# Masking the second score pass of a fused attention tower on GpSimd instead of TensorE

## The reference, cut to what matters

```
# token layer, 4 times (band: a query sees keys within W = 64 positions)
scores = where(allowed, q.k / sqrt(16), -1e9);  probs = softmax(scores);  a = probs @ v
h = layer_norm(h + a @ Wo + bo);  h = layer_norm(h + gelu(h @ W1 + b1) @ W2 + b2)
# causal attention on layer_norm(h): q and k rotated, then
att = where(key <= query, q.k / 4, -inf);  y = softmax(att) @ v;  h = h + y @ W_proj + b_proj
# experts: top-k by gate score, silu(x Wg) * (x Wu) @ Wd, scattered and added; plus the shared branch
```

## Time and profile before

| what | value |
|---|---|
| median of three runs | 7495.74 us (7485.59 to 7497.77) |
| profiled execution, its own time | 7492.35 us |
| span of its trace | 7490.6 us, mean granted TensorE clock 0.967 |
| PE busy | 6488.7 us, 87% of the span |
| DVE busy | 4520.8 us, 60% |
| ACT busy | 2636.2 us, 35% |
| POOL busy | 1088.9 us, 15% |
| DMA | 25 GB/s over the span |

### The profile page before, as it was taken

One profiled execution on the slowest core, in us unless ns is written; L12 is line 12 of the kernel. 1 busy time (PEld: TensorE's weight loads), 2 busy tenths in 40 slices (PEclk: granted clock), 3 DMA queues, 4 the chain that ended last, 5 costly groups with the idle time before them and its releaser, 6 DMA issues. The chain is left out here.

```text
span 7490.6 us, 145369 instructions
## 1 busy us (share of the span) xinstructions
PE 6488.7 (87%) x54482; PEld 4986.5 (67%) x54482; DVE 4520.8 (60%) x11626; ACT 2636.2 (35%) x4677; POOL 1088.9 (15%) x1089
## 2 busy tenths in 40 slices
PE   1999999999999999999999999978888886279999
PEld 1777777777777777777777777756666664256766
DVE  6666666666666666666666666656666665732222
ACT  0444444444444444444444444433333332001111
POOL 4000000000000000000000000011111110133333
PEclk9999999999999999999999999989999998589999
DMA  5000000100000100000000000000000000023332
GB/s 99 15 14 14 14 14 14 29 14 14 14 14 14 29 14 14 14 14 14 19 25 14 14 14 14 14 28 17 17 16 18 16 17 17 0 61 84 69 83 52
DMA packets 195770, 185.94 MB, mean 25 GB/s; under 512 B 44402, under 2 KB 181268, under 8 KB 195668
## 3 DMA queue, kind: packets, MB, share of 16 engines
q1 hardware_dynamic: 168020, 147.84, 6.6%
q0 software_dynamic: 27648, 36.72, 3.1%
HBM read 124.23 MB, written 60.26 MB: 25 GB/s over the span
## 5 line engine op out<-in xcount | busy, mean ns | idle before, releaser
L684 ACT ACTIVATE pT<-bank 128x384 f32<-128x384 f32 x1920 | 857.9, 489 | 1184.0 <-PE bank L509 1184.0
L861 DVE TENSOR_REDUCE mx<-bank 128x2 f32<-128x384 f32 x1548 | 813.1, 554 | 497.5 <-PE bank L483 497.5
L481 PE MATMUL bank<-maskb,eyeb 128*128 128x384 bf16 x1932 | 641.9, 332 | 197.0 <-DVE mx L861 67.7
L578 PE MATMUL bank<-hT,w 96*128 96x256 f32 x3072 | 770.9, 387 | 43.5 <-ACT hT L704 43.5
L507 PE MATMUL bank<-maskb,eyeb 128*128 128x384 bf16 x1920 | 634.9, 331 | 54.6 <-ACT pT L684 49.2
L483 PE MATMUL bank<-kT,qT 128*128 128x192 bf16 (+2 forms) x3864 | 638.5, 247 | 0.0
L509 PE MATMUL bank<-qT,kT 128*128 128x192 bf16 (+2 forms) x3840 | 629.3, 246 | 0.0
L578 PEld LDWEIGHTS bank<-hT,w 96*128 96x128 f32 x3072 | 542.6, 190 | 125.4 <-ACT hT L704 72.6
L468 PE MATMUL bank<-eyeb,stack 128*128 128x128 bf16 x7728 | 541.1, 227 | 70.3 <-DVE stack L847 70.3
L468 PEld LDWEIGHTS bank<-eyeb,stack 128*128 128x128 bf16 x7728 | 489.6, 102 | 104.1 <-DVE stack L847 80.7
L590 PE MATMUL bank<-w,pT 128*128 128x192 f32 x3072 | 533.5, 330 | 0.0
(11 more groups left out here) (203 smaller groups left out, 11160.0 us busy)
## 6 DMA issues: line engine op xcount, KB each, us to landing
hcur<-hbuf SPq DMA_DIRECT2D x165, 192.0 KB, 2.4
hbuf<-hout SPq DMA_DIRECT2D x128, 192.0 KB, 2.0
amb<-am_d SPq DMA_DIRECT2D x131, 128.0 KB, 2.9
exp_wg<-in_ewg SPq DMA_DIRECT2D x16, 768.0 KB
exp_wu<-in_ewu SPq DMA_DIRECT2D x16, 768.0 KB
exp_wd<-in_ewd SPq DMA_DIRECT2D x16, 576.0 KB
xs<-xr SPq DMA_DIRECT2D x32, 272.0 KB, 2.2
hbuf<-emb_z SPq DMA_DIRECT2D x17, 384.0 KB
```

Of the source, the lines that this page charges most:

```text
L481: nc.tensor.matmul(dst[:, 0:SCOLS], eyeb[:], maskb[:, masks, :], start=True, stop=False)
L578: last = nc.tensor.matmul(bank[s][f // 2][:, (f % 2) * S:(f % 2 + 1) * S], w1[:, c, f * P:(f + 1) * P], hT[s][:, c, :], start=(c == 0), st ...
L684: ph.inc(nc.scalar.activation(pT[s][:, h % NPT, :], bank[s][h % 2][:, 0:SCOLS], ACT.Exp, scale=SCALE), "p", s)
L861: last = nc.vector.tensor_reduce(mx[s][:, :, h], src[:, 0:SCOLS].rearrange("p (t k) -> p t k", t=T), AX, ALU.max)
```

## The change

The mask matmul of the second pass goes, in both kinds of layer, so the two score matmuls open and close their own accumulation. The exponential is then also taken of scores that are masked, relative to a maximum over the unmasked ones. On POOL a new function `pool_keep` zeroes the masked entries of `pT` in place, for four heads at a time, with `affine_select`, an instruction that compares an affine expression of partition and column with zero and keeps the entry or writes 0.0. For a band group these are four instructions (64, 128, 128 and 64 columns, times four heads); for a causal group two (128 columns, times four heads). Three groups stand between POOL's front part (L1045) and its rstd (L1050). A new key "kept" counts groups, and `pe_products` waits for it in place of "p". In the order of PE the products are set later: group 0 after head 8, group 1 after head 11, group 2 between fill 1 and fill 2, and the output transposes between fill 3 and fill 4. The number of slots of `pT` (8), the banks, the first score pass and its mask matmuls stay.

```
-            nc.tensor.matmul(dst[:, 0:SCOLS], eyeb[:], maskb[:, masks + 1, :], start=True, stop=False)
             for t, (c0, f0, w) in enumerate(kcols):
                 last = nc.tensor.matmul(dst[:, c0:c0 + w], kT[s][:, h, t * P:(t + 1) * P],
-                                        qT[s][:, h, f0:f0 + w], start=False, stop=(t == T - 1))
+                                        qT[s][:, h, f0:f0 + w], start=True, stop=True)
...
-            ph.wait(pe, "p", s, K.it, 4 * g + 4)
+            ph.wait(pe, "kept", s, K.it, g + 1)
...
-                if K and h >= 3 + LAG and (h - 3 - LAG) % 4 == 0:
-                    pe_products(ph, pe, K, (h - 3 - LAG) // 4, kcols)
+                if K and h in (8, 12):
+                    pe_products(ph, pe, K, h // 4 - 2, kcols)
             for f in range(6):
                 if K and f == 2:
+                    pe_products(ph, pe, K, 2, kcols)
+                if K and f == 4:
                     pe_output(ph, pe, K)
...
+        def pool_keep(ph, pool, K, g, causal):
+            s = K.s
+            ph.wait_apart(pool, "p", s, K.it, 4 * g + 4, half_ok, 1)
+            pool.wait_ge(half_ok, 1)
+            p = pT[s][:, (4 * g) % NPT:(4 * g) % NPT + 4, :]
+            def keep(x, n, w, key, base):
+                return nc.gpsimd.affine_select(x, x, [[0, n], [-key, w]], ALU.is_ge, 0.0, base=base, channel_multiplier=key)
+            if causal:
+                keep(p[:, :, 0:P], 4, P, -1, 0)
+                last = keep(p[:, :, 2 * P:3 * P], 4, P, -1, 0)
+            else:
+                keep(p[:, :, 0:W], 4, W, -1, W)
+                keep(p[:, :, W:3 * W], 4, P, 1, 0)
+                keep(p[:, :, 3 * W:5 * W], 4, P, -1, 0)
+                last = keep(p[:, :, 5 * W:6 * W], 4, W, 1, 0)
+            ph.inc(last, "kept", s)
...
             if K:
+                for g in range(3):
+                    pool_keep(ph, pool, K, g, causal)
                 s = K.s
                 ph.wait(pool, "var1", s, K.it)
```

More of the change, by code:

```diff
@@ L414, in tower @@
             h_in=16, hT_ps=1, hT=1, qk_ps=2, v_ps=1, qk=2, v=1, stk=1, fill=6, ev_v=3, ev_s=3,
-            sc1=NH, mx=NH, m=1, mT_ps=3, mT=3, sc2=NH, p=NH, pv=NH, ot=1, otT_ps=2, att=1,
+            sc1=NH, mx=NH, m=1, mT_ps=3, mT=3, sc2=NH, p=NH, kept=3, pv=NH, ot=1, otT_ps=2, att=1,
             aT_ps=1, aT=1, wo_ps=1, var1=1, rstd1=1, h1=1, h1T_ps=1, h1T=1)
@@ L497, in pe_maxima, with pe_scores2 @@
                 ph.inc(last, "mT_ps", s)
-        def pe_scores2(ph, pe, K, h, masks, kcols):
+        def pe_scores2(ph, pe, K, h, kcols):
             s = K.s
@@ L633, in tensor_half @@
                 if K and h < NH:
-                    pe_scores2(ph, pe, K, h, masks, kcols)
+                    pe_scores2(ph, pe, K, h, kcols)
                 if F and h == plan.input:
```

## The result

The changed kernel takes 8074.48 us, median of four runs (8065.84 to 8083.34), against 7493.85 us before; the ratio is 1.0776, 95% interval 1.0758 to 1.0795. The forecast was 8095 us. Its profiled span is 8064.1 us, 573.5 us more than before.

What follows compares the result with a forecast made beforehand. PE, busy 87% of the span, was taken as the bound, with DVE's stack chain nearly tied. 2.3 + 1.4 + 0.6 us a token half gave 550 us, the causal layer 48: 8095 us, range 7600 to 8650.

Steps and rivals of the forecast that it cites:

- The floor: Token half with masks that cost nothing: first score at t = 17.27 against 17.48, a gain of 0.2 us, not 2.0.
- K: Time of POOL's four selects for one band group (1536 elements a partition): 2.8 us, range 1.6 to 4.0.
- The chain by t: Token half: group 0 kept at 7.7, group 2 starts at 13.4, first score 6.35 us later at 19.75, 2.3 us late.
- Contention: Token half: POOL's keeps and DVE operations with two SBUF inputs hold each other up, 1.4 us, bounds 0 and 2.7.
- Clock: Token half: PE's granted clock falls after standing ahead of groups 0 and 2, costing 0.6 us, from 0 up to 2.3.
- Sum of the token layers: 2.3 + 1.4 + 0.6 = 4.3 us a token half, x 128 = 550 us slower.
- The causal layer: Group 0 starts at 10.1, group 2 at about 15.4; fills already late, so 1.5 us a half (0.5 to 3), 48 us.

Runs made afterwards that it cites:

- no_keep: The changed kernel without its affine selects, products waiting for the exponentials, late order kept; 7521.08 us, ratio 1.0043 to the kernel before.
- keeps_first: The changed kernel with the three keeps ahead of the front's residual on POOL; 8180.01 us, ratio 1.0971 to the kernel before.
- keeps_aside: The changed kernel with the selects working on a separate tile that no product waits for; 8176.54 us, ratio 1.0915 to the kernel before.
- pow_wait: The changed kernel with each group's selects replaced by tiny POOL powers, PE still waiting for them; 8010.94 us, ratio 1.0694 to the kernel before.
- quarter_keeps: The changed kernel with each select on one head of its four, same instructions and waits; 7532.01 us, ratio 1.0101 to the kernel before.
- warm_first: The changed kernel with 8 idle matmuls ahead of PE's wait for group 0; 8137.01 us, ratio 1.0854 to the kernel before.
- two_heads: The kernel before, early order, with only heads 0 and 1's second-pass masks moved to one early POOL keep; 7432.88 us, ratio 0.9920 to before.

## Why the prediction was right, and where it wasn't

**The floor** (a gain of 0.2 us a token half at best): right, and along the forecast's own path. `no_keep` shows 0.01 for the half; its fill 0 starts at t = 9.84 (9.85 forecast), product group 2 at 10.84 (10.92) and the first score at 17.15 (17.27).

**K.** Forecast 2.8 us a band group, without contention. Measured 2.43 for the third group of the half shown and 2.93 for the first two (5.85 / 2), but both lie beside DVE's work; a group that DVE nearly leaves alone takes 2.18 us (`keeps_first`, group 0). Single selects with nothing of DVE beside them take about 0.23 us for 64 elements, 0.29 for 128, 0.41 for 256 and 0.63 for 512: 0.9 ns an element and a fixed 0.18 us. So the fixed 0.2 us read off the adds was right and the 1.3 ns an element was too much. That the whole came near the contended group is luck, for the forecast then added contention on top. (The Trainium skill's "roughly line-rate" for one input, "GPSIMD Engine Reference", section 4.1, gave 2.1 us; the undisturbed group agrees to 4%.)

**The chain by t.** Group 0 forecast for 7.8, measured 7.97; group 2 forecast for 13.4 plus a contention of 1.4, measured 14.02; from there to the first score 6.35 forecast, 6.31 measured. That path, read off rows 4 and 5 gap by gap, was the most exact part of the sum, at full clock; in the other kind of half it takes 6.82 us.

**Contention.** The mechanism is shown by `keeps_aside` and `pow_wait`; the bookkeeping wasn't right. I let only DVE operations with two SBUF inputs stand against POOL, but the casts (741 against 561 ns) and above all the small bf16 copies (413 against 253) stretch as well: of 1.8 us that the stack chain grew in the half shown, 0.64 are those of the six copies (1.74 us in its timeline against 1.10). And I added it to POOL's chain alone. It is on both: by the undisturbed 2.18 us a group, POOL's three groups grew by 1.7 us in the half shown (5.85 + 2.43 against 6.54), and DVE's chain by 1.8. In the other kind of half DVE's chain is the one that PE meets, which the forecast has no path for. Because the two chains end so close together, one sum for either came out about right, and that is luck too. (The Trainium skill, "SBUF — State Buffer", section "SBUF: two separate sides", counts VectorE instructions in a 2-port mode among those that contend with GpSimd, and says that whoever comes second blocks for the whole instruction. The records agree: the copies of `keeps_aside` that begin under a select end 0.11 to 0.12 us after it. In the change 413 ns is a mean of copies that met one, up to 709 ns, and of others that fell into POOL's pause; the median is 254.)

**Clock.** 0.6 us forecast. Up to the first score the half shown lost 2.85 us and the other kind 3.76. Behind fill 0 the clock takes 1.3 us of the latter and nothing that can be read of the former, 0.65 on average. The stretch at 0.50 ahead of fill 0 is not in that, so the whole is somewhat more. The mean half lost 3.68; what is missing from 3.3, the mean of the two, lies mostly behind the first score and isn't explained.

**Sum of the token layers.** 4.3 forecast, 3.68 measured: 550 against 471 us.

**The causal layer is the step that failed.** I took 1.5 us a half, with bounds of 0.5 and 3; it is 3.27. The first score comes at t = 23.33 against 20.05. The timeline in the changed kernel (t = 0 at 5703.06) answers to the earlier trace rows:

```profile
5711.17 4.07 POOL L1042 TENSOR_SCALAR_AFFINE_SELECT pT<-pT 128x512 f32<-128x512 f32 x4
...
5713.18 1.51 PE L526 MATMUL bank<-pT,vaug 128*32 128x256 f32 x16 [3.22 <-POOL pT L1042]
...
5716.63 1.97 DVE L846 COPY stack<-stack 128x384 bf16<-128x384 bf16 x6
...
5718.79 1.89 PE L468 MATMUL bank<-eyeb,stack 128*128 128x128 bf16 x16 [1.14 <-DVE stack L848]
...
5720.60 1.51 PE L526 MATMUL bank<-pT,vaug 128*32 128x256 f32 x16
```

Group 0 comes at t = 10.1, as forecast. But I reasoned that the fills are late anyway and would swallow the rest. The stack chain, which makes them late, is itself held up by the selects: fill 0 starts at t = 15.73 in place of 13.79. And product group 2, which used to run ahead of PE's wait for that chain, now stands behind it and behind fills 0 and 1, at half clock: from 5720.60 to the next fill at 5722.05 it is 1.4 us of path where it was free. 1.9 + 1.4 = 3.3. But that the second term is the step's is an account of this one half. `quarter_keeps` has the same order, and its causal half corrects it:

```profile
5714.96 1.07 PE L468 MATMUL bank<-eyeb,stack 128*128 128x128 bf16 x16 [0.35 <-DVE stack L848]
...
5715.95 0.86 PE L526 MATMUL bank<-pT,vaug 128*32 128x256 f32 x16
```

Fill 0 starts at t = 13.78, where it did before, PE has not stood long ahead of it, and the granted clock is at 1.00 all through the fills. The moved step is 0.8 us of path (5715.95 to 5716.74), and still the first score starts at t = 19.91, 0.14 us sooner than before, where the fills begin at a clock of 0.50. From fill 0 to the first score it is 6.13 us, and 7.60 in the change. So of the 3.28 us in the change 1.94 are the stack chain's, held up by the selects, and the rest is the clock: at full clock the late order costs nothing against the kernel before. The forecast's causal sum had contention on POOL's chain alone, and no term for the clock. This cost 32 x 1.8 = 57 us over the forecast, and the token layers' excess of 79 us in it hid that: the total, 8095 against 8074, looks more exact than its terms are.

## What to carry to other kernels

Before taking work off the busiest engine, follow the next chain: here half the masks' time in the token layers lay beside DVE's stack chain, and the order needed to make room for the new engine gave back the other half. Work moved to GpSimd isn't free because GpSimd is idle 85% of the time: if it streams through SBUF it lengthens VectorE's SBUF work beside it, so put it where VectorE isn't on the path, and move only as much as pays (two heads of twelve: 0.8% gained, more than half of it by the clock; twelve: 7.8% lost). When a step is moved behind a wait, charge its full length there, at the clock that the wait leaves, and charge the steps around it at that clock too.

## What the runs showed of the hardware that I had not expected

- Affine selects of POOL on f32 in place: 1536 elements in four instructions in 2.18 us when VectorE nearly leaves them alone (`keeps_first`), 2.43 to 3.00 beside it; single ones with nothing of VectorE beside them 0.23 us for 64 elements (`quarter_keeps`) and 0.63 for 512.
- Bf16 copies of 384 elements from SBUF to SBUF on DVE stretch most beside them: 253 ns alone, 413 in the change, 534 in `warm_first`, 630 in `keeps_first`. A different tile (`keeps_aside`, 497) doesn't help; POOL instructions of 2 elements (`pow_wait`, 253) don't hurt. A copy that begins under a select ends 0.11 us after it (574 copies of `keeps_aside`).
- After the same wait of PE of 1.8 us for the stack chain the granted clock fell to 0.50 in the kernel before and stayed at 1.00 in 19 of 30 causal halves of `two_heads`, which is worth 1.5 us in such a half.
- Idle matmuls ahead of a wait raised the clock and still made the kernel slower, because a faster PE took away the pause in which DVE ran free.
